# Attention on one Trainium2 core: the output projection as three fp32r passes over high and low parts, its tiles spread over two groups

## The chip, the cores and the metric

The kernel runs on one core of one Trainium2 chip. The metric is device time in microseconds for one execution, inputs and outputs in DRAM. TensorE (PE), VectorE (DVE), ScalarE (ACT), GpSimd (POOL) and SyncE (SP, which only issues DMAs here) run side by side, each through its own list of instructions in order, and wait for one another by semaphores.

## The reference

A macaron block on x of 2 x 2048 rows of 512 floats: half a mixture-of-experts layer, attention, half a mixture-of-experts layer, each behind a layer norm and added to x. Only the attention is touched:

```python
q = (x @ Wq + bq).reshape(b, s, 16, 32).transpose(0, 2, 1, 3)
k = x @ Wk + bk                      # one head of 32 for all 16 query heads
v = x @ Wv + bv
attn = softmax(einsum('bhsd,btd->bhst', q, k) / sqrt(32), axis=-1)
out = einsum('bhst,btd->bhsd', attn, v).transpose(0, 2, 1, 3).reshape(b, s, 512)
return out @ Wo + bo
```

## The kernel before

Attention is one unrolled program (`attention`). The 4096 rows are 8 chunks c of QT = 512 queries; the 16 heads are GPC = 4 groups g of HG = 4 heads. G = 4c + g counts the 32 groups. A group goes over its batch's 2048 keys in STEPS = 16 steps of 128, two steps to a pair (phase) p = 0 to 7.

In phase p TensorE makes eight score blocks (`scores`, L1776, fp32r, 128 keys x 512 queries of a head) and, in turn with them, eight blocks of the row maxima of the groups to come (`maxima`, L1797, fp32r). Then follow, where they are due, the transposed shifts (L1815, phase 6), an output tile (`output`, L1807), the denominators (L1836, phase 4), and at the end of the phase the values of the two steps before (`values`, L1825, fp32, into pO). Block maxima, shifts, output tiles and denominators take turns in pM, a ring of RING = 4 PSUM banks: each waits in `bank_free` until the bank's user four places earlier has been read. With eight maxima a phase, a shift, a tile or a denominator is a phase's ninth bank user and waits for the fifth maximum of its phase.

ACT takes the exponential of each score block (L1744). POOL adds the probabilities of two steps in two halves of 128x1024, both inputs in SBUF (`add_pair`, L1691), and between the halves of most pairs issues a DMA that accumulates the sum of an earlier pair (`bring`, L1707). In pair 1 it also normalises the output of the group before the last one (L1720). DVE reduces each block maximum out of PSUM (L1914), and at the end of its phase does, in this order of the code: copy_o (L1941, phase 0: pO of the group before to SBUF), make_shifts (phase 5: L1924 and L1925 reduce the maxima to one value a row, one in fp32 and one rounded to fp32r; L1928 subtracts the two, 128x16, all in SBUF), copy_shift (phase 6), the addition of an output tile to xo (L1919), the denominators' copy (phase 4) and their reciprocal (phase 6). The shifts go through the transposes of phase 6 into qT of the next group.

A chunk's output is four tiles of 128 rows, each the sum over the four groups of o_n[g] (fp32, 128x128 weights) times Wo[g] (128x512). They stand in the group g = 1 of the next chunk, in phases 4 to 7. The tiles of the last chunk (`last_output`, L1857) come at the end of the program. SP stores a finished chunk and loads the next rows (`store_x`, `load_x`) in the group g = 2, ahead of the DMAs that carry the denominators (`reciprocals`).

Numbers such as "(1,6)" below mean group g = 1, phase 6. The query projection ahead of attention (L1268 to L1270) already multiplies by three fp32r passes: high x high, low x high, high x low.

Of the kernel before, what the change touches and what calls it, by code (L numbers as in the profile page):

```python
# [38 lines left out]
def begin(eng, *sems):  # L39
    for s in sems:  # L40
        eng.sem_inc(s, A)  # L41
# [1391 lines left out]
def attention(nc, tag, k, prep, wo, q_d, d_d, sums, xb_d, x_out):  # L1433
# [8 lines left out]
    with ExitStack() as ctx:  # L1442
# [40 lines left out]
        FIRST_BLOCKS = (11, 11, 11, 11, 10, 10)  # L1483
        OUT_PAIRS = (4, 5, 6, 7)
        SUM_PAIR = 4
# [13 lines left out]
        pair = [m.sb(f"pair{b}", [P, HG * QT]) for b in range(MOVED)]  # L1499
        o_new = m.sb("o_new", [P, QT])  # L1500
        o_n = [m.sb(f"o_n{g}", [P, QT]) for g in range(GPC)]
        d_sb = m.sb("d", [P, QT])
# [9 lines left out]

        s_wo = m.sem("wo")
        s_xl = m.sem("xl")
        s_xs = m.sem("xs")
# [25 lines left out]

        def o_raw(g):
            return o_new if g == 0 else o_n[g]

        def blocks_in(G, k):
# [9 lines left out]
        def output_in(G, k):  # L1555

            return OUT_PAIRS.index(k) if G % GPC == 1 and G > GPC and k in OUT_PAIRS else None

# [29 lines left out]
        def last_out(t):  # L1588

            return pM[:, (END + t) % RING, :] if t < RING - 1 else pS[:, 0, :]  # L1590
# [4 lines left out]
        with nc.Block() as block:  # L1595
# [66 lines left out]
            def _(pool):  # L1662
# [47 lines left out]
                def normalise(c, g):  # L1710
                    G = GPC * c + g
                    pool.wait_ge(s_oc, A + G + 1)
                    pool.sem_inc(k["pool_on"], 1)
                    pool.wait_ge(s_ri, A + 64 * (G + 1))
                    pool.sem_inc(k["pool_on"], 1)
                    if g == 0 and not (isinstance(c, int) and c == 0):

                        pool.wait_ge(s_mr, A + outputs_done[c - 1])
                        pool.sem_inc(k["pool_on"], 1)
                    pool.tensor_tensor(o_n[g][:, :], o_raw(g)[:, :], d_rec[:, :], ALU.mult).then_inc(s_on, 1)  # L1720

# [11 lines left out]
            def _(act):  # L1733
                begin(act, s_ex, s_sha)

# [10 lines left out]
                def copy_shift(G, g, h):  # L1746
                    if h == 2:
                        act.wait_ge(s_x, A + G + 1)
                    act.activation(qT[g][3 * DH:4 * DH, h, :], pM[h * DH:(h + 1) * DH, shift_at[G] % RING, :], ACT.Copy
                                   ).then_inc(s_sha, 1)  # L1750

                for h in (2, 3):
                    copy_shift(0, 0, h)
                for G in range(GROUPS):
                    for t in range(STEPS):
                        for h in range(HG):
                            exponential(G, t, h)
                        if t == 2 * COPY_PAIR + 1 and G + 1 < GROUPS:
                            for h in (2, 3):
                                copy_shift(G + 1, (G + 1) % GPC, h)  # L1760

            @block.tensor
            def _(pe):
# [36 lines left out]
                def output(r, c, t):  # L1800

                    bank_free(r)
                    if t == 0:
                        pe.wait_ge(s_wo, A + 16)
                        pe.wait_ge(s_on, A + GPC * (c + 1))
                    for g in range(GPC):
                        ins = pe.matmul(pM[:, r % RING, :], o_n[g][:, t * P:(t + 1) * P], wo_sb[:, g, :],  # L1807
                                        start=g == 0, stop=g == GPC - 1)
                    ins.then_inc(s_mp, 1)
# [38 lines left out]
                def last_output(t, groups):  # L1848

                    if t == HG - 1 and 0 in groups:  # L1850
                        pe.wait_ge(s_ex, A + GROUPS * (STEPS * HG))
                    if t == 0 and 0 in groups:
                        pe.wait_ge(s_on, A + GROUPS - 1)
                    if GPC - 1 in groups:
                        pe.wait_ge(s_lon, A + t + 1)
                    for g in groups:
                        ins = pe.matmul(last_out(t), o_n[g][:, t * P:(t + 1) * P], wo_sb[:, g, :], start=g == 0,  # L1857
                                        stop=g == GPC - 1)
                    if GPC - 1 in groups:
                        ins.then_inc(s_mp, 1)  # L1860

# [46 lines left out]
            def _(dve):  # L1908
                begin(dve, s_mr, s_mx, s_shift, s_shd, s_dc, s_rec, s_oc, s_lrec, s_lon)

# [27 lines left out]
                def copy_o(c, g):  # L1938

                    dve.wait_ge(s_pv, A + (GPC * c + g + 1) * STEPS)  # L1940
                    dve.tensor_copy(o_raw(g)[:, :], pO[:, :]).then_inc(s_oc, 1)  # L1941

# [11 lines left out]
                def phase(G, p):  # L1954
# [5 lines left out]
                    if p == 0 and G > 0:  # L1960
                        copy_o(*divmod(G - 1, GPC))
                    if p == SHIFT_PAIR and G + 1 < GROUPS:
                        make_shifts(G + 1, count)
# [17 lines left out]
                for G in range(GROUPS):  # L1981
                    for p in range(PAIRS):
                        phase(G, p)
                dve.wait_ge(s_lsum, A + PAIRS)
                dve.wait_ge(s_ri, A + 64 * (GROUPS - 1))
# [3 lines left out]
                def last_quarter(t):  # L1989
# [3 lines left out]
                    if t == 0:  # L1993
                        dve.wait_ge(s_pv, A + GROUPS * STEPS)
                    dve.tensor_tensor(o_n[GPC - 1][:, part], pO[:, part], d_rec[:, part], ALU.mult).then_inc(s_lon, 1)

# [73 lines left out]
```

## Time and profile before

| | us |
|---|---|
| median of 3 runs | 3182.35 (3176.6 to 3187.31) |
| the profiled execution | 3182.29 |
| its span, first to last instruction | 3180.6 |
| attention in it | about 820 to 2509 |
| TensorE busy, of the span | 2770.0 (87%) |
| POOL | 2218.7 (70%) |
| DVE | 2046.3 (64%) |
| ACT | 1522.7 (48%) |

The shares of the whole span mix three stages. In attention TensorE is busy nearly throughout; the experts before and after it are bound otherwise and are not touched. A matmul record lasts from its start to the end of its way through the array, so records that follow each other overlap: the distance of their starts is what one costs.

### The profile page before, as it was taken

To read this page: it belongs to the slowest core of one execution; us is meant where nothing else is said; L and a number is where in the kernel's file an instruction comes from. 1 tells how busy PE (TensorE), PEld (TensorE's weight loads), DVE (VectorE), ACT (ScalarE), POOL (GpSimd) and SP (SyncE) were. 2 spreads that over 40 slices of the span, in tenths; PEclk is the share of its full clock that TensorE was granted. 3 is DMA by queue.
4 is the path that set the end of the run, shared out by engine and by line. 5 is a ranking of instruction groups with operands and counts; after the bars stand their busy time and mean duration, and the time that the engine had idled before them with its cause. 6 is when DMAs were issued, how large, how long until landed. Compare 5 with 4: busy or idle time off the path is not lost. (4 is left out here: it accounts for less than half of the span.)

```text
span 3180.6 us, 44938 instructions
## 1 busy us (share of the span) xinstructions
PE 2770.0 (87%) x15264; PEld 1651.1 (52%) x15264; DVE 2046.3 (64%) x3922; ACT 1522.7 (48%) x2871; POOL 2218.7 (70%) x1430
## 2 busy tenths in 40 slices
PE   7967777388899999999999999999999776888870
PEld 4644444166455555555555555555554464555540
DVE  7843222267788878788787887887874394333334
ACT  5522222153466656566566665665656351222220
POOL 2248888462489879799798897997978323777770
PEclk9978888689999999999999999999999877999995
DMA  5669999895377777678676776776766364999998
GB/s 211 220 198 244 237 241 242 184 272 189 83 157 161 144 159 147 137 170 160 143 162 134 167 144 139 164 150 155 148 135 140 121 219 135 212 236 240 236 184 322
DMA packets 216987, 575.78 MB, mean 181 GB/s; under 512 B 33980, under 2 KB 35004, under 8 KB 192824
## 3 DMA queue, kind: packets, MB, share of 16 engines
q0 software_dynamic: 87296, 343.98, 53.7%
q1 hardware_dynamic: 125240, 220.55, 21.4%
q10 hardware_dynamic: 4224, 8.39, 0.7%
q8 instruction: 123, 2.02, 0.3%
q14 instruction: 104, 0.85, 0.1%
HBM read 230.94 MB, written 155.24 MB: 121 GB/s over the span
## 5 line engine op out<-in xcount | busy, mean ns | idle before, releaser
L1914 DVE TENSOR_REDUCE attention_mx<-attention_pM 128x1 f32<-128x512 f32 x1984 | 1209.3, 682 | 197.0 <-PE attention_pM L1797 196.3
L1744 ACT ACTIVATE attention_prob<-attention_pS 128x512 f32<-128x512 f32 x2048 | 1032.7, 624 | 592.2 <-PE attention_pS L1776 591.8
L1691 POOL TENSOR_TENSOR attention_pair<-attention_prob 128x1024 f32<-128x1024 f32 x380 | 949.6, 2504 | 210.0 <-ACT attention_prob L1744 199.3
L1776 PE MATMUL attention_pS<-attention_qT,prep_kT 128*128 128x512 f32 x2048 | 840.6, 412 | 3.1 <-ACT attention_prob L1744 2.2
L1797 PE MATMUL attention_pM<-prep_kT,attention_qT 96*128 96x512 f32 x1984 | 788.2, 398 | 1.8 <-DVE attention_mx L1914 1.1
L1776 PEld LDWEIGHTS attention_pS<-attention_qT,prep_kT 128*128 128x128 f32 x2048 | 387.5, 190 | 308.9 <-issue 210.2
L1825 PE MATMUL attention_pO<-attention_prob,attention_v 128*32 128x512 f32 x4096 | 491.7, 598 | 0.0
L768 POOL DMA_INDIRECT sum<-experts_res,c_table x256 | 403.7, 1577 | 125.4 <-issue 79.4
L1797 PEld LDWEIGHTS attention_pM<-prep_kT,attention_qT 96*128 96x128 f32 x1984 | 377.9, 190 | 92.0 <-DVE attention_mx L1914 16.5
L752 POOL DMA_INDIRECT experts_rows<-xn_rows,c_table x256 | 250.7, 979 | 103.8 <-issue 70.1
L797 PE MATMUL experts_pT<-c_ident,experts_rows 128*128 128x128 f32 x1024 | 169.8, 307 | 120.8 <-issue 46.8
L943 DVE TENSOR_SCALAR experts_res<-experts_pD,experts_rows 128x512 f32<-128x512 f32 x128 | 93.5, 749 | 272.8 <-DMA sum<-experts_res,c_table 173.4
L1825 PEld LDWEIGHTS attention_pO<-attention_prob,attention_v 128*32 128x32 f32 x4096 | 110.1, 109 | 252.4 <-issue 155.6
L1691 POOL TENSOR_TENSOR prep_acc<-attention_prob 128x1024 f32<-128x1024 f32 x68 | 165.7, 2449 | 88.6 <-ACT attention_prob L1744 84.1
L797 PEld LDWEIGHTS experts_pT<-c_ident,experts_rows 128*128 128x128 f32 x1024 | 141.0, 209 | 155.8 <-issue 105.4
L922 DVE COPY experts_xT<-experts_pT 128x512 f32<-128x512 f32 x128 | 88.3, 690 | 198.7 <-PE experts_pT L797 133.5
L892 ACT ACTIVATE experts_res<-experts_pD,experts_rows 128x512 f32<-128x512 f32 x128 | 85.3, 686 | 257.6 <-DMA sum<-experts_res,c_table 191.2
L309 POOL TENSOR_TENSOR route_eqp<-route_eq,route_count 128x1536 f32<-128x1536 bf16 (+1 forms) x16 | 48.2, 3012 | 201.7 <-ACT route_count L429 201.7
L1691 POOL TENSOR_TENSOR attention_acc<-attention_prob 128x1024 f32<-128x1024 f32 x64 | 156.7, 2473 | 6.5 <-POOL attention_pair L1691 3.5
L884 ACT ACTIVATE experts_sg<-experts_pU 128x256 f32<-128x256 f32 x80 | 30.7, 384 | 267.8 <-PE experts_pU L814 119.8
L878 ACT ACTIVATE experts_xT<-experts_pT 128x512 f32<-128x512 f32 x128 | 76.5, 597 | 108.4 <-PE experts_pT L797 63.3
L814 PE MATMUL experts_pU<-experts_xT,experts_wup 128*64 128x256 f32 x1024 | 123.2, 395 | 1.0 <-issue 1.0
(181 smaller groups left out, 3135.1 us busy)
## 6 DMA issues: line engine op xcount, KB each, us to landing
prep_acc<-attention_pair POOLq DMA_DIRECT2D x96, 1024.0 KB, 7.6
attention_acc<-attention_pair POOLq DMA_DIRECT2D x90, 1024.0 KB, 7.3
attention_qT<-q_parts SPq DMA_DIRECT2D x96, 256.0 KB
xn_rows<-route_xn SPq DMA_DIRECT2D x16, 1152.0 KB, 6.6
experts_wup<-in_L_ffn_w_up_dram SPq DMA_DIRECT2D x64, 256.0 KB
q_parts<-prep_acc SPq DMA_DIRECT2D x64, 256.0 KB, 4.3
ahead_wup<-in_L_ffn_w_up_dram SPq DMA_DIRECT2D x64, 256.0 KB, 9.0
combine_got<-sum SPq DMA_DIRECT2D x16, 1024.0 KB
```

The costliest lines, as they stand in the source:

```text
L752: pool.indirect_dma_start(rows[e % RING][:, a * HALVES + h, :], None, xn_d, bass.IndirectOffsetOnAxis(ap=k["table"][:, 2 * e + a, h:h + 1] ...
L768: pool.indirect_dma_start(sums[a], bass.IndirectOffsetOnAxis(ap=k["table"][:, 2 * e + a, h:h + 1], axis=0), res[e % 2][:, a, h, :], None, ...
L797: t = pe.transpose(pT[:, half, o:o + P], rows[e % RING][:, a * HALVES + h, c:C:CK], k["ident"][:, :])
L814: t = pe.matmul(pU[n % 2][a * H:(a + 1) * H, v, :], wts[b][0][:, a, c, v * H:(v + 1) * H], xT[e % 2][:, c, a, :], start=c == 0, stop=c == ...
L922: dve.tensor_copy(xT[e % 2][:, 2:4, a, :], pT[:, 1, :].rearrange("p (c n) -> p c n", c=2)).then_inc(s_cd, 1)
L943: dve.tensor_scalar(res[e % 2][:, 1, h, :], pD[:, h, 1, :], rows[e % RING][:, HALVES + h, C + 2 * e + 1:C + 2 * e + 2], None, ALU.mult).th ...
L1691: pool.tensor_tensor(to[:, part], prob[2 * n % PROBS][:, part], prob[(2 * n + 1) % PROBS][:, part], ALU.add).then_inc(s_pair, 1)
L1744: act.activation(prob[t % PROBS][:, h * QT:(h + 1) * QT], pS[:, at, :], ACT.Exp).then_inc(s_ex, 1)
L1776: pe.matmul(pS[:, n % 3, :], kT[:, key:key + P], qT[g][:, h, :], start=True, stop=True).then_inc(s_sc, 1)
L1797: pe.matmul(pM[:, r % RING, :], qT[g][0:3 * DH, h, t * P:(t + 1) * P], kT[0:3 * DH, key:key + 512], start=True, stop=True).then_inc(s_mp, 1)
L1825: ins = pe.matmul(pO[h * DH:(h + 1) * DH, :], v_sb[:, batch * STEPS + t, :], prob[t % PROBS][:, h * QT:(h + 1) * QT], start=t == 0, stop=t ...
L1914: dve.tensor_reduce(mx[:, unit, part:part + 1], pM[:, r % RING, :], X, ALU.max).then_inc(s_mr, 1)
```

## The change

o and Wo are each split into a high part (rounded to fp32r by ACT) and a low part (the rest, subtracted by DVE and rounded to fp32r). An output tile becomes, for each of four groups, high x high + low x high + high x low, 12 fp32r matmuls in place of 4 fp32 ones. Wo is split once, in the groups G = 1 and 2. The normalised o of group G - 2 is split in group G, high after the exponentials of pair 4, low behind the maxima of phase 5 ahead of the shifts. The four tiles stand at (1,6), (1,7), (2,0), (2,1) instead of (1,4) to (1,7). copy_o writes into one of two buffers `raw` and waits for POOL's normalising of two groups before; POOL normalises in place and no longer waits for the outputs of the chunk before, which ACT now does. At the end the first three groups of a tile are split, the last one stays fp32.

```diff
@@ -1481,7 +1481,8 @@
         FIRST_BLOCKS = (11, 11, 11, 11, 10, 10)
-        OUT_PAIRS = (4, 5, 6, 7)
+        OUT_PAIRS = ((1, 6), (1, 7), (2, 0), (2, 1))
+        HIGH_PAIR, LOW_PAIR = 4, 5
         SUM_PAIR = 4
@@ -1497,8 +1498,12 @@
         pair = [m.sb(f"pair{b}", [P, HG * QT]) for b in range(MOVED)]
-        o_new = m.sb("o_new", [P, QT])
-        o_n = [m.sb(f"o_n{g}", [P, QT]) for g in range(GPC)]
+        raw = [m.sb(f"raw{b}", [P, QT]) for b in range(2)]
+        o_hi = [prep[n][:, :, :].rearrange("p c n -> p (c n)") for n in ("wkvh", "wkvl")]
+        o_hi += [m.sb(f"o_hi{b}", [P, QT], F32R)[:, :] for b in range(2)]
+        wo_hi, wo_lo = prep["wqh"], prep["wql"]
+        o_lo = [m.sb(f"o_lo{g}", [P, QT], F32R) for g in range(GPC)]
+        o_last = m.sb("o_last", [P, QT])
         d_sb = m.sb("d", [P, QT])
@@ -1554,7 +1560,8 @@
-            return OUT_PAIRS.index(k) if G % GPC == 1 and G > GPC and k in OUT_PAIRS else None
+            at = (G % GPC, k)
+            return OUT_PAIRS.index(at) if G > GPC + 1 - (at[0] == 1) and at in OUT_PAIRS else None
@@ -1713,11 +1720,7 @@
                     pool.sem_inc(k["pool_on"], 1)
-                    if g == 0 and not (isinstance(c, int) and c == 0):
-
-                        pool.wait_ge(s_mr, A + outputs_done[c - 1])
-                        pool.sem_inc(k["pool_on"], 1)
-                    pool.tensor_tensor(o_n[g][:, :], o_raw(g)[:, :], d_rec[:, :], ALU.mult).then_inc(s_on, 1)
+                    pool.tensor_tensor(raw[G % 2][:, :], raw[G % 2][:, :], d_rec[:, :], ALU.mult).then_inc(s_on, 1)
@@ -1748,6 +1751,18 @@
                                    ).then_inc(s_sha, 1)
+
+                def high_wo(g):
+                    if g == 0:
+                        act.wait_ge(s_wo, A + 16)
+                    act.activation(wo_hi[:, g, :], wo_sb[:, g, :], ACT.Copy).then_inc(s_woh, 1)
+
+                def high(G):
+                    c, g = divmod(G, GPC)
+                    act.wait_ge(s_on, A + G + 1)
+                    if c > 0:
+                        act.wait_ge(s_mr, A + outputs_done[c - 1])
+                    act.activation(o_hi[g], raw[G % 2][:, :], ACT.Copy).then_inc(s_oh, 1)
@@ -1755,9 +1770,14 @@
                             exponential(G, t, h)
+                        if G == 1 and t % 2 == 1 and t < 2 * GPC:
+                            high_wo(t // 2)
+                        if t == 2 * HIGH_PAIR + 1 and G > 1:
+                            high(G - 2)
                         if t == 2 * COPY_PAIR + 1 and G + 1 < GROUPS:
                                 copy_shift(G + 1, (G + 1) % GPC, h)
+                high(GROUPS - 2)
@@ -1801,11 +1821,14 @@
                     if t == 0:
-                        pe.wait_ge(s_wo, A + 16)
-                        pe.wait_ge(s_on, A + GPC * (c + 1))
+                        pe.wait_ge(s_wol, A + GPC)
+                        pe.wait_ge(s_ol, A + GPC * (c + 1))
+                    own = slice(t * P, (t + 1) * P)
                     for g in range(GPC):
-                        ins = pe.matmul(pM[:, r % RING, :], o_n[g][:, t * P:(t + 1) * P], wo_sb[:, g, :],
-                                        start=g == 0, stop=g == GPC - 1)
+                        pe.matmul(pM[:, r % RING, :], o_hi[g][:, own], wo_hi[:, g, :], start=g == 0, stop=False)
+                        pe.matmul(pM[:, r % RING, :], o_lo[g][:, own], wo_hi[:, g, :], start=False, stop=False)
+                        ins = pe.matmul(pM[:, r % RING, :], o_hi[g][:, own], wo_lo[:, g, :], start=False,
+                                        stop=g == GPC - 1)
                     ins.then_inc(s_mp, 1)
@@ -1849,15 +1872,18 @@
                         pe.wait_ge(s_ex, A + GROUPS * (STEPS * HG))
+                    own = slice(t * P, (t + 1) * P)
                     if t == 0 and 0 in groups:
-                        pe.wait_ge(s_on, A + GROUPS - 1)
-                    if GPC - 1 in groups:
-                        pe.wait_ge(s_lon, A + t + 1)
+                        pe.wait_ge(s_ol, A + GROUPS - 1)
                     for g in groups:
-                        ins = pe.matmul(last_out(t), o_n[g][:, t * P:(t + 1) * P], wo_sb[:, g, :], start=g == 0,
-                                        stop=g == GPC - 1)
-                    if GPC - 1 in groups:
-                        ins.then_inc(s_mp, 1)
+                        if g < GPC - 1:
+                            pe.matmul(last_out(t), o_hi[g][:, own], wo_hi[:, g, :], start=g == 0, stop=False)
+                            pe.matmul(last_out(t), o_lo[g][:, own], wo_hi[:, g, :], start=False, stop=False)
+                            pe.matmul(last_out(t), o_hi[g][:, own], wo_lo[:, g, :], start=False, stop=False)
+                        else:
+                            pe.wait_ge(s_lon, A + t + 1)
+                            pe.matmul(last_out(t), o_last[:, own], wo_sb[:, g, :], start=False, stop=True
+                                      ).then_inc(s_mp, 1)
@@ -1937,8 +1963,22 @@
-                    dve.wait_ge(s_pv, A + (GPC * c + g + 1) * STEPS)
-                    dve.tensor_copy(o_raw(g)[:, :], pO[:, :]).then_inc(s_oc, 1)
+                    G = GPC * c + g
+                    dve.wait_ge(s_pv, A + (G + 1) * STEPS)
+                    if G > 1:
+                        dve.wait_ge(s_on, A + G - 1)
+                        dve.sem_inc(k["dve_on"], 1)
+                    dve.tensor_copy(raw[G % 2][:, :], pO[:, :]).then_inc(s_oc, 1)
+
+                def low_wo(g):
+                    dve.wait_ge(s_woh, A + g + 1)
+                    dve.tensor_tensor(wo_lo[:, g, :], wo_sb[:, g, :], wo_hi[:, g, :].bitcast(F32), ALU.subtract
+                                      ).then_inc(s_wol, 1)
+
+                def low(G):
+                    dve.wait_ge(s_oh, A + G + 1)
+                    dve.tensor_tensor(o_lo[G % GPC][:, :], raw[G % 2][:, :],
+                                      o_hi[G % GPC].bitcast(F32), ALU.subtract).then_inc(s_ol, 1)
@@ -1959,6 +1999,10 @@
                         copy_o(*divmod(G - 1, GPC))
+                    if G == 2 and p < GPC:
+                        low_wo(p)
+                    if p == LOW_PAIR and G > 1:
+                        low(G - 2)
                     if p == SHIFT_PAIR and G + 1 < GROUPS:
@@ -1981,6 +2025,7 @@
                         phase(G, p)
+                low(GROUPS - 2)
                 dve.wait_ge(s_lsum, A + PAIRS)
@@ -1992,7 +2037,7 @@
                         dve.wait_ge(s_pv, A + GROUPS * STEPS)
-                    dve.tensor_tensor(o_n[GPC - 1][:, part], pO[:, part], d_rec[:, part], ALU.mult).then_inc(s_lon, 1)
+                    dve.tensor_tensor(o_last[:, part], pO[:, part], d_rec[:, part], ALU.mult).then_inc(s_lon, 1)
```

## Rows read from the trace of the kernel before

**Rows 1.** Windows view: busy us (count) by engine, granted clock, DMA share, GB/s
```profile
1200.00:1500.00 300.00, 300.00 (x1655) 169.37 (x1654) 252.19 (x427) 195.56 (x388) 259.30 (x137) 1.00 0.73 151
```

**Rows 2.** Source view of L1941, 1064 to 1284: count, ns, first to last start
```profile
L1941 DVE COPY attention_o_new<-attention_pO x1: 691/691/691, 1080.5 to 1080.5; 128x512 f32<-128x512 f32 x1
...
L1941 DVE COPY attention_o_n<-attention_pO x3: 691/692/692, 1143.6 to 1240.9; 128x512 f32<-128x512 f32 x3
```

**Rows 3.** Source view of L1807: weight loads of the output tiles
```profile
L1807 PEld LDWEIGHTS attention_pM<-attention_wo,attention_o_n x224: 186/190/190, 1101.7 to 2389.6; 128*128 128x128 f32 x112
```

**Rows 4.** Timeline (start us, us, what), TensorE: seven fp32r passes in a row
```profile
811.64 0.40 PE L1270 MATMUL attentionp_pQ<-attentionp_xh,prep_wql 128*128 128x512 f32 x1
...
813.04 0.40 PE L1270 MATMUL attentionp_pQ<-attentionp_xh,prep_wql 128*128 128x512 f32 x1
```

**Rows 5.** Timeline, TensorE: a tile of today, and an ordinary phase
```profile
1131.85 0.39 PE L1797 MATMUL attention_pM<-prep_kT,attention_qT 96*128 96x512 f32 x1
...
1132.15 3.70 PE L1807 MATMUL attention_pM<-attention_wo,attention_o_n 128*128 128x512 f32 x8
...
1143.77 0.40 PE L1797 MATMUL attention_pM<-prep_kT,attention_qT 96*128 96x512 f32 x1
...
1147.37 1.92 PE L1825 MATMUL attention_pO<-attention_prob,attention_v 128*32 128x512 f32 x16
```

**Rows 6.** Timeline, VectorE, at the end of phase 0 of a group 2
```profile
1143.57 0.69 DVE L1941 COPY attention_o_n<-attention_pO 128x512 f32<-128x512 f32 x1 [0.28 <-PE attention_pO L1825]
...
1144.21 4.88 DVE L1914 TENSOR_REDUCE attention_mx<-attention_pM 128x1 f32<-128x512 f32 x8
```

**Rows 7.** Groups by line and form: the last tiles, busy us, mean ns
```profile
L1857 PE MATMUL attention_pM<-attention_wo,attention_o_n 128*128 128x512 f32 x24 | 11.0, 601 | 0.0
```

**Rows 8.** Timeline, ScalarE, behind pair 4, with the idle time before
```profile
1168.86 4.03 ACT L1744 ACTIVATE attention_prob<-attention_pS 128x512 f32<-128x512 f32 x8 [3.48 <-PE attention_pS L1776]
```

**Rows 9.** Timeline of SyncE's DMA queue in a group 2
```profile
1144.88 0.43 SPq L1610 DMA_DIRECT2D sum<-attention_xo  x1
...
1156.29 0.38 SPq L1604 DMA_DIRECT2D attention_xo<-x_rows  x1
...
1167.46 1.26 SPq L1618 DMA_DIRECT2D d_parts<-attention_d  x4
```

**Rows 10.** Source view of L1366, a VectorE addition with two SBUF inputs
```profile
L1366 DVE TENSOR_TENSOR attentionp_got<-attentionp_got,attentionp_other x8: 681/688/1153, 625.7 to 647.6; 128x512 f32<-128x512 f32 x8
```

**Rows 11.** Timelines, VectorE then GpSimd, end of phase 5, usual group
```profile
1174.01 0.22 DVE L1924 TENSOR_REDUCE attention_whole<-attention_mx 128x16 f32<-128x64 f32 x1
...
1174.39 0.21 DVE L1928 TENSOR_TENSOR attention_shift<-attention_whole,attention_shift 128x16 f32<-128x16 f32 x1
...
1174.89 4.88 DVE L1914 TENSOR_REDUCE attention_mx<-attention_pM 128x1 f32<-128x512 f32 x8 [0.29 <-PE attention_pM L1797]
...
1172.18 2.38 POOL L1691 TENSOR_TENSOR attention_pair<-attention_prob 128x1024 f32<-128x1024 f32 x1 [1.91 <-ACT attention_prob L1744]
...
1175.09 2.70 POOL L1691 TENSOR_TENSOR attention_pair<-attention_prob 128x1024 f32<-128x1024 f32 x1
```

**Rows 12.** Timelines, VectorE, GpSimd, TensorE: phase 6 of G = 0; usual phase
```profile
866.14 2.38 DVE L1928 TENSOR_TENSOR attention_shift<-attention_whole,attention_shift 128x16 f32<-128x16 f32 x1
...
868.45 4.86 DVE L1914 TENSOR_REDUCE attention_mx<-attention_pM 128x1 f32<-128x512 f32 x8
...
865.80 2.67 POOL L1691 TENSOR_TENSOR attention_pair<-attention_prob 128x1024 f32<-128x1024 f32 x1
...
863.82 1.92 PE L1825 MATMUL attention_pO<-attention_prob,attention_v 128*32 128x512 f32 x16
...
872.16 1.92 PE L1825 MATMUL attention_pO<-attention_prob,attention_v 128*32 128x512 f32 x16
...
1172.26 1.92 PE L1825 MATMUL attention_pO<-attention_prob,attention_v 128*32 128x512 f32 x16
...
1178.61 1.92 PE L1825 MATMUL attention_pO<-attention_prob,attention_v 128*32 128x512 f32 x16
```

More of the change, by code:

```diff
@@ L1513, in attention @@
         s_wo = m.sem("wo")
+        s_woh = m.sem("woh")
+        s_wol = m.sem("wol")
+        s_oh = m.sem("oh")
+        s_ol = m.sem("ol")
         s_xl = m.sem("xl")
@@ L1540, in attention @@
         s_shd = m.sem("shd")
-        def o_raw(g):
-            return o_new if g == 0 else o_n[g]
         def blocks_in(G, k):
@@ L1733, in _ @@
             def _(act):
-                begin(act, s_ex, s_sha)
+                begin(act, s_ex, s_sha, s_woh, s_oh)
                 def exponential(G, t, h):
@@ L1908, in _ @@
             def _(dve):
-                begin(dve, s_mr, s_mx, s_shift, s_shd, s_dc, s_rec, s_oc, s_lrec, s_lon)
+                begin(dve, s_mr, s_mx, s_shift, s_shd, s_dc, s_rec, s_oc, s_lrec, s_lon, s_wol, s_ol)
                 def maxima(r, count, n):
```

## The prediction

> **What bounds the kernel now.** I read the stages first, then the groups inside attention, then one phase instruction by instruction. In a 300 us stretch of attention TensorE is busy for all 300 us at a granted clock of 1.00 (its 2.4 GHz level), POOL for 259, DVE for 252, ACT for 196 [rows 1]. So the matmul stream sets the time, and a microsecond taken from it counts only as long as nothing makes it wait. The copies of pO out of PSUM (L1941) mark the groups: 1080.5 to 1143.6 is the group that carries the four output tiles, 63.1 us; the next two take 97.3/2 = 48.65 us each [rows 2]. A tile therefore costs (63.1 - 48.65)/4 = 3.61 us of the bound today, and there are 224/8 = 28 such tiles in the groups (224 weight loads, one a record) [rows 3], besides four at the end.
>
> **The passes.** A tile is 8 matmul records now (an fp32 matmul runs as two) and 12 fp32r passes afterwards. fp32r passes stand back to back in the query projection: six starts in 813.04 - 811.64 = 1.40 us, 0.233 us each, though each record lists 0.40 [rows 4]. So 12 x 0.233 = 2.80 us. The tile also waits for its bank: the present one starts 0.30 us after the last block maximum instead of 0.233 [rows 5], 0.07 us; the weight load behind such a wait is in the open, somewhere between nothing and its 0.19 us [rows 3]. I take 0.08, near the low end, since a load normally runs ahead of its matmul. A tile then costs 2.95 us (2.80 to 3.06) and saves 0.66 us (0.55 to 0.81).
>
> **Moving tiles to group 2.** In (1,6), (1,7) and (2,0) nothing else is late, 0.66 each. At (2,0) DVE adds the tile only after copy_o, which waits for the phase's values, where copy_o is now followed at once by the next phase's maxima, 0.64 us later [rows 6]. With an addition in between (0.6 us, the distance of such instructions) and the new semaphore increment (0.06, my estimate, between 0 and 0.1) the maxima of phase 1 start 0.66 us late. TensorE makes a maximum every 0.467 us and DVE takes 4.88/8, about 0.6; four banks cover this within a phase, but the ninth bank user of the phase, the tile (2,1), waits for the fifth maximum: today 1144.21 + 4 x 0.6 + 0.69 = 1147.30 against 1147.37, when TensorE goes on [rows 5, 6]. There is no slack: what DVE loses there, TensorE loses. So (2,1) saves nothing. Per chunk 3 x 0.66 = 2.0, in seven chunks 13.9 us (0 lost there and 0.81 saved: 22.7; 0.55 and a loss of 0.2: 10). The last tiles run 24 of their 32 records as 36 passes: 24 records take 11.0 us today [rows 7], 36 x 0.233 are 8.4, at most 2.6 saved, less the changes between the two kinds; I take 1.3 (0 to 2.6).
>
> **The high parts on ACT.** One 128x512 copy at the end of pair 4 of each group from G = 2, about 0.6 us as ACT's eight exponentials take 4.03: ACT has 3.48 us idle right there [rows 8]. Cost nothing; without that cover 30 x 0.6 = 18 us. Its new wait for the chunk's earlier outputs, formerly POOL's, is met by pair 1 of group 2, three pairs before. Behind it only exponentials queue. The four of Wo, once, lie in idle time as well: ACT is busy for only 196 of 300 us [rows 1].
>
> **The queues.** SP's store of a chunk now waits for tile (2,1) rather than being ready when SP gets there. Today it is issued at 1144.88 and over by 1156.29, 11.4 us; SP is next needed for the denominators at 1167.46 [rows 9]. The tile's addition would come at about 1149.2 + 2 x 2.95 + 0.7 + 0.9 = 1156.7, the store end at 1168.1, while the denominators move by 6.6 to 1174.1. Six microseconds are left, cost nothing. POOL's normalising keeps its place and loses a wait that never came last.
>
> **The low parts on DVE: here the time goes.** low() is put behind the maxima of phase 5, ahead of make_shifts, in G = 2 to 30 (29 groups with a phase 6 that makes shifts). It is a subtraction of 128x512 with both inputs in SBUF; a like one takes 0.68 us unhindered [rows 10]. What matters is what POOL does then. In phase 5 the maxima end at about 1173.97, just ahead of L1924 at 1174.01; L1924, with one input, runs its 0.22 us in the middle of POOL's addition of 1172.18 to 1174.56; L1928, the only instruction there with two SBUF inputs, ends at 1174.60, 0.04 us after that addition [rows 11]. That might be chance, but in G = 0, whose phases bring more maxima, DVE comes later: L1928 comes at 866.14, POOL's addition has been running since 865.80 and ends at 868.47, and an instruction of 0.2 us takes 2.38 and ends at 868.52. The maxima behind it begin at 868.45, TensorE waits for a bank, and that phase lasts 872.16 - 863.82 = 8.34 us against 1178.61 - 1172.26 = 6.35 in a usual group [rows 12]: 1.99 us lost. Undisturbed, the maxima start 1174.89 - 1172.26 = 2.63 us after the values, here at 866.45: 2.00 late on DVE is 1.99 on TensorE. Phase 6 too has a ninth bank user, the transposes.
>
> Now the new order. low() is ready at about 1173.9, inside the addition that ends at 1174.56, and is held to about 1174.5; with 0.6 us to go it ends near 1175.1. L1924 and L1925 follow at about 1175.05 and 1175.2, L1928 is ready at 1175.4. POOL's second half addition starts at 1175.09 and lasts 2.70 [rows 11], perhaps 0.1 later because of low(). L1928 misses the gap of half a microsecond between POOL's two additions in which it gets through today, and ends at about 1177.85. The next maxima start near 1177.8 instead of 1174.89: 2.9 us late, all of it TensorE's. 29 x 2.9 = 84 us. Bounds: 2.0, the one case measured (58 us), and 3.1 if POOL itself is pushed back by 0.2 (90 us). I take 2.9, since it is read from the place itself.
>
> The Trainium skill, page "SBUF — State Buffer", section "Who interferes with whom", says of this that a VectorE instruction with two SBUF inputs contends with a GpSimd instruction that reads SBUF, and that whichever starts second is blocked to the end of the first. The rows above agree; read alone, the rule would let each of the two instructions wait up to a whole POOL addition, 29 x (2.4 + 2.7) = 148 us; the places of the rows make it 84.
>
> low_wo(), four times in G = 2, has two SBUF inputs too. By the same gaps I put 0.5 us on each, 2 us (0 to 8).
>
> **The sum**, against the profiled execution of 3182.3 us (its span is 3180.6; the median of the runs is 3182.35, so nothing is to be converted): 3182.3 - 13.9 - 1.3 + 84 + 2 = 3253 us. With the bounds: 3182.3 - 25.4 + 58 = 3215 and 3182.3 - 10 + 90 + 8 = 3270.
>
> **The rivals.**
> - B, L1928 still slips in ahead of POOL's second addition. It would have to be ready by 1175.1 instead of 1175.4. Then the shifts end near 1175.6 and the maxima come 0.66 us late: 29 x 0.66 = 19; 3182.3 - 15.2 + 19 + 2 = 3188 us. Against it: at 866.14 it was 0.34 us behind and was held [rows 12].
> - C, the other side: low() is not held at all, because two inputs are not what holds L1928. Then low() adds about 0.5 us, L1928 is ready at 1174.9, in the gap ahead of 1175.09, and the maxima start 0.22 late, after the 0.29 us that DVE idles there now [rows 11]: 6.4 us. 3182.3 - 15.2 + 6.4 + 1 = 3174 us. It decides at 1175.09. The end of L1928 with POOL's, at both places, speaks against it.
> - D, low() and the shifts cost nothing and the cheap end of the tiles holds: 3182.3 - 25 = 3157 us. The 0.29 us of idle time against a subtraction of 0.6 speaks against it.
> - E, low() is passed over at the first addition's end and both wait for the second: it ends at 1178.4, L1928 at 1178.95, 4.0 us late, 116 us; 3285 us. The gap of half a microsecond with low() already waiting speaks against it.
> - The passes could fail to be cheaper, at the 0.40 us that a record lists: 12 x 0.40 = 4.8 us, 28 x 1.2 = 34 us more. The starts in the query projection exclude that [rows 4].
>
> **How the numbers follow.** Forecast 0.76, B 0.08, C 0.07, D 0.04, E 0.05. The range takes in the forecast with its bounds and E: 3215 to 3286, 0.81 together. About 0.3% (9.5 us) is what a measurement can tell from no change. Slower by more is the forecast and E, 0.81. B and most of C lie within it, 0.13. D and the rest of C are faster, 0.06.
>
> **What would show it.** In the changed kernel the tile is 12 passes in about 2.8 us, the groups with tiles about 5 to 6 us longer than the others, all groups from G = 2 about 2.9 us longer in phase 6; L1928's successor takes over 2 us in nearly every group instead of 0.21 and ends with a POOL addition; TensorE, never idle before, waits about 1 us or more for a maximum in each phase 6. If L1928 stays at 0.2 us, the main term is wrong and B, C or D holds. If the subtraction itself shows over 2 us, it is E.

## The result

The changed kernel takes 3262.1 us (median, 3254.7 to 3267.6) against 3183.4 for the kernel before: ratio 1.0248, 95% interval 1.0221 to 1.0276. The forecast was 3253 us, in a range of 3215 to 3286, and slower with a chance of 0.81. The profiled execution's span is 3262.0 us against 3180.6.

The profile's page and the views that group waits and lines already name the place. These are the page's line of busy times; the group of the block maxima on TensorE, busy us and mean ns, then the idle time before and its releaser; the group of the shifts' subtraction on DVE; and the wait as a total with its count and longest case:

```profile
PE 2802.7 (86%) x15388; PEld 1688.7 (52%) x15388; DVE 2147.4 (66%) x3957; ACT 1551.6 (48%) x2906; POOL 2218.6 (68%) x1430
...
L1817 PE MATMUL attention_pM<-prep_kT,attention_qT 96*128 96x512 f32 x1984 | 808.1, 408 | 59.4 <-DVE attention_mx L1940 58.7
...
L1954 DVE TENSOR_TENSOR attention_shift<-attention_whole,attention_shift 128x16 f32<-128x16 f32 x32 | 72.7, 2271 | 1.1
...
PE attention_pM L1817 <- DVE attention_mx L1940: 58.7, 30, 2.5
```

L1817 is the old L1797, L1940 the old L1914, L1954 the old L1928. TensorE, busy for all of a 300 us stretch before [rows 1], now waits 30 times for a block maximum: 1.15 us in G = 0, 2.47 in G = 2 behind the low part of Wo, and 1.96 to 1.97 in phase 6 of each of G = 2 to 29; and the subtraction of 128x16, 0.21 us in a usual group before [rows 11], takes 2.27 us on average. One such place, the end of phase 5 in G = 7, as timelines (start us, us, what) of DVE, POOL and TensorE:

```profile
1241.35 1.22 DVE L1980 TENSOR_TENSOR attention_o_lo<-attention_raw,prep_wkvl 128x512 fp32r<-128x512 f32 x1
1242.49 0.20 DVE L1950 TENSOR_REDUCE attention_whole<-attention_mx 128x16 f32<-128x64 f32 x1
1242.61 0.21 DVE L1951 TENSOR_REDUCE attention_shift<-attention_mx 128x16 fp32r<-128x64 f32 x1
1242.86 2.40 DVE L1954 TENSOR_TENSOR attention_shift<-attention_whole,attention_shift 128x16 f32<-128x16 f32 x1
1245.18 4.86 DVE L1940 TENSOR_REDUCE attention_mx<-attention_pM 128x1 f32<-128x512 f32 x8
...
1239.64 2.37 POOL L1698 TENSOR_TENSOR attention_pair<-attention_prob 128x1024 f32<-128x1024 f32 x1 [1.91 <-ACT attention_prob L1747]
1241.96 0.85 POOL L1714 DMA_DIRECT2D attention_acc<-attention_pair  x1
1242.55 2.65 POOL L1698 TENSOR_TENSOR attention_pair<-attention_prob 128x1024 f32<-128x1024 f32 x1
...
1239.72 1.92 PE L1848 MATMUL attention_pO<-attention_prob,attention_v 128*32 128x512 f32 x16
...
1245.91 0.50 PE L1817 MATMUL attention_pM<-prep_kT,attention_qT 96*128 96x512 f32 x1 [1.96 <-DVE attention_mx L1940]
...
1248.89 1.92 PE L1848 MATMUL attention_pO<-attention_prob,attention_v 128*32 128x512 f32 x16
```

Set beside rows 11 and 12: the low part (L1980) is ready while POOL's first addition runs and takes 1.22 us instead of about 0.68. The shifts' subtraction then comes after the first addition's end (1242.01) and ends at 1245.26, 0.06 us after the second one's. The maxima start at 1245.18; 2.63 us after the values, as in a usual group before, would have been 1242.35. Phase 6 lasts 1248.89 - 1239.72 = 9.17 us against 6.35 before [rows 12]: 2.82 us lost. L1951, which writes as small a tile but has one input, runs its 0.21 us while the second addition runs; only the subtraction with two inputs is held.

The distance of the copies of pO measures a group, as in rows 2. In the changed kernel (L1971) a usual group and then one with tiles, by first and last start:

```profile
L1971 DVE COPY attention_raw<-attention_pO x2: 692/692/692, 1043.4 to 1094.9; 128x512 f32<-128x512 f32 x2
...
L1971 DVE COPY attention_raw<-attention_pO x2: 692/692/692, 1094.9 to 1155.3; 128x512 f32<-128x512 f32 x2
```

Values in us, read from the starts of the copies in DVE's timeline (groups in which the granted clock stayed at 1.00, but for G = 2 and e4's g = 2):

| kernel | usual group | with tiles, g = 1 | g = 2 | G = 2 |
|---|---|---|---|---|
| before | 48.7 | 63.07 | 48.7 | 48.68 |
| changed | 51.5 | 60.34 | 55.15 | 58.29 |
| e2_shifts_first | 48.90 | 57.78 | 52.55 | 53.37 |
| e4_subtraction_alone | 51.5 | 63.07 | 52.40 | 52.40 |
| f0_split_one_phase_earlier | 48.69 | 57.54 | 52.34 | 53.81 |
| f1_tiles_apart | 48.69 | 57.51 | 51.74 | 53.83 |
| f3_wo_on_pool | 48.69 | 57.51 | 51.73 | 48.84 |

In e4 the granted clock fell to half behind the wait of phase 6 in each of the groups G = 2, 6, 10, 14, 18, 22 and 26 and in no other; with this go the 0.9 us by which its g = 2 lies above its usual group. In the changed kernel the groups G = 1 to 30 together are 85.3 us longer than before, what lies ahead of them is 1.7 us shorter, and the end of attention, from the last copy of pO to the last addition to xo, is 2.1 shorter: 81.5 of the span's 81.4.

### The profile page after: what moved, and what is told of

It is laid out like the page before. It is cut to its first block and busy times, and to the rows that moved or that the text cites. A ratio compares the mean times of both kernels' runs of the same rounds, so it can differ in the third digit from the quotient of the medians.

```text
span 3262.0 us, 45309 instructions
## 1 busy us (share of the span) xinstructions
PE 2802.7 (86%) x15388; PEld 1688.7 (52%) x15388; DVE 2147.4 (66%) x3957; ACT 1551.6 (48%) x2906; POOL 2218.6 (68%) x1430
## 5 line engine op out<-in xcount | busy, mean ns | idle before, releaser
L1747 ACT ACTIVATE attention_prob<-attention_pS 128x512 f32<-128x512 f32 x2048 | 1043.5, 623 | 632.8 <-PE attention_pS L1796 632.0
L1940 DVE TENSOR_REDUCE attention_mx<-attention_pM 128x1 f32<-128x512 f32 x1984 | 1208.7, 683 | 191.1 <-PE attention_pM L1817 190.6
L1817 PE MATMUL attention_pM<-prep_kT,attention_qT 96*128 96x512 f32 x1984 | 808.1, 408 | 59.4 <-DVE attention_mx L1940 58.7
L1817 PEld LDWEIGHTS attention_pM<-prep_kT,attention_qT 96*128 96x128 f32 x1984 | 381.0, 192 | 184.9 <-DVE attention_mx L1940 112.9
```

Of the source, the lines that this page charges most:

```text
L1747: act.activation(prob[t % PROBS][:, h * QT:(h + 1) * QT], pS[:, at, :], ACT.Exp).then_inc(s_ex, 1)
L1817: pe.matmul(pM[:, r % RING, :], qT[g][0:3 * DH, h, t * P:(t + 1) * P], kT[0:3 * DH, key:key + 512], start=True, stop=True).then_inc(s_mp, 1)
L1940: dve.tensor_reduce(mx[:, unit, part:part + 1], pM[:, r % RING, :], X, ALU.max).then_inc(s_mr, 1)
```

## The experiments

The theory: while an addition of POOL with both inputs in SBUF runs, a DVE instruction with two SBUF inputs is held. The low part is held to the end of the first addition, which makes the shifts' subtraction miss its way past POOL, and it is held to the end of the second. The rivals: the 0.6 us of DVE work as such; the place of the split; the passes and their tiles. The diffs show the lines that matter; the allocation of spare tiles and code that only moves along are left out.

**e4: the subtraction alone.** The kernel before, with nothing of the change but a subtraction of the same size into a spare tile:

```diff
+                    if p == SHIFT_PAIR and G > 1:
+                        dve.wait_ge(s_wo, A + 16)
+                        dve.tensor_tensor(spare[:, :], wo_sb[:, 0, :], wo_sb[:, 1, :], ALU.subtract)
                     if p == SHIFT_PAIR and G + 1 < GROUPS:
                         make_shifts(G + 1, count)
```

> The kernel before with one thing added: in phase 5 of G = 2 to 31, ahead of the shifts, a DVE subtraction of 128x512 with two inputs in SBUF into a spare tile. Nothing else of the change. Theory: in the 22 groups without tiles the shifts' subtraction takes 2.3 us and TensorE loses 2.9 us: 64 us; in the 7 groups with tiles phase 5 carries a tile, whose time covers the wait; 3182 + 64 = 3246 us, some more if the clock falls behind the waits. Rival (passes, split on ACT, moved tiles are the cause): 3182 us.

3245.3 us against 3177.1 for the kernel before in the same series: ratio 1.0217 (1.0200 to 1.0234). The groups of DVE's lines, count, busy us and mean ns:

```profile
L1929 DVE TENSOR_TENSOR attention_shift<-attention_whole,attention_shift 128x16 f32<-128x16 f32 x32 | 72.8, 2274 | 1.1
...
L1965 DVE TENSOR_TENSOR attention_spare<-attention_wo 128x512 f32<-128x512 f32 x30 | 38.1, 1268 | 0.1
```

The two instructions last as in the changed kernel. Usual groups grow by 2.82 us, the groups with tiles by nothing: there the subtractions are held just as long (1.19 and 2.42 us at 1121.30 and 1122.79), but the tile at (1,5) gives DVE the time. With nothing else of the change the kernel loses 68 us, most of the change's 79.

**e2: the same work, behind the shifts.**

```diff
-                    if p == LOW_PAIR and G > 1:
-                        low(G - 2)
                     if p == SHIFT_PAIR and G + 1 < GROUPS:
                         make_shifts(G + 1, count)
+                    if p == LOW_PAIR and G > 1:
+                        low(G - 2)
```

> The changed kernel with the low part still in phase 5, but behind the shifts instead of ahead of them; the same DVE work ahead of the maxima of phase 6. Theory: the shifts' subtraction gets through at the end of POOL's first addition as before (0.2 us), the low part follows in the gap ahead of the second addition and ends about 0.35 us after TensorE's next maximum is ready; 29 x 0.35 = 10 us, 3182 - 15 + 7 + 10 = 3184 us. Rival (DVE's 0.6 us more of work in front of phase 6 is the cause, not POOL): no better than the change, 3250 to 3265 us.

3174.6 us, ratio to before 0.9992 (0.9983 to 1.0002). The same place, DVE then POOL:

```profile
1273.04 0.22 DVE L1954 TENSOR_TENSOR attention_shift<-attention_whole,attention_shift 128x16 f32<-128x16 f32 x1
1273.17 0.68 DVE L1980 TENSOR_TENSOR attention_o_lo<-attention_raw,attention_o_hi 128x512 fp32r<-128x512 f32 x1
1273.78 4.86 DVE L1940 TENSOR_REDUCE attention_mx<-attention_pM 128x1 f32<-128x512 f32 x8
...
1270.84 2.37 POOL L1698 TENSOR_TENSOR attention_pair<-attention_prob 128x1024 f32<-128x1024 f32 x1 [1.91 <-ACT attention_prob L1747]
1273.15 0.86 POOL L1714 DMA_DIRECT2D prep_acc<-attention_pair  x1
1273.74 2.70 POOL L1698 TENSOR_TENSOR attention_pair<-attention_prob 128x1024 f32<-128x1024 f32 x1
```

The shifts' subtraction waits at the first addition's end and gets through (0.22 us), and the low part straight behind it goes too, unheld at 0.68 us. A usual group is 48.90 us, 0.20 longer than before, not the 0.35 that I had expected. By the medians 87 us of the changed kernel's time come from the order of two instructions (81 by the two ratios, since the time of the kernel before differs between the series; 88 by the lengths of the groups G = 1 to 30 in the traces). The rival of the DVE work as such falls.

**e3: one SBUF input in the low part's place.**

```diff
-                    dve.tensor_tensor(o_lo[G % GPC][:, :], raw[G % 2][:, :],
-                                      o_hi[G % GPC].bitcast(F32), ALU.subtract).then_inc(s_ol, 1)
+                    dve.bn_stats(one[:, :], raw[G % 2][:, :]).then_inc(s_ol, 1)
```

> The changed kernel with the subtraction of the low part of o replaced by an instruction of the same length with one input in SBUF (row statistics of the same tile), at the same place; the low part of o is left out of the result (its tiles are filled once). Theory: it isn't held, takes 0.68 us, the shifts' subtraction is ready at about 0.15 us ahead of POOL's second addition and takes 0.2 us; maxima 0.2 us late, 29 x 0.2 = 6; 3182 - 15 + 7 + 6 = 3180 us. Rival (DVE's time alone): as the change, 3250 to 3265 us. If the shifts' subtraction just misses the gap, its rows show 2.3 us and the time is near 3255 us.

3261.4 us, ratio 1.0265 (1.0248 to 1.0282): no better. DVE, then POOL, in G = 8; then the same around a low part of Wo in G = 2:

```profile
1295.21 0.68 DVE L1981 BATCH_NORM_STATS2 attention_one<-attention_raw 128x6 f32<-128x512 f32 x1
...
1296.17 2.96 DVE L1955 TENSOR_TENSOR attention_shift<-attention_whole,attention_shift 128x16 f32<-128x16 f32 x1
...
1293.50 2.37 POOL L1699 TENSOR_TENSOR attention_pair<-attention_prob 128x1024 f32<-128x1024 f32 x1 [1.91 <-ACT attention_prob L1748]
1295.82 0.86 POOL L1715 DMA_DIRECT2D prep_acc<-attention_pair  x1
1296.41 2.67 POOL L1699 TENSOR_TENSOR attention_pair<-attention_prob 128x1024 f32<-128x1024 f32 x1
...
955.36 0.68 DVE L1976 TENSOR_TENSOR prep_wql<-attention_wo,prep_wqh 128x512 fp32r<-128x512 f32 x1
...
952.95 2.38 POOL L1699 TENSOR_TENSOR attention_pair<-attention_prob 128x1024 f32<-128x1024 f32 x1 [2.85 <-ACT attention_prob L1748]
955.27 0.85 POOL L1715 DMA_DIRECT2D prep_acc<-attention_pair  x1
```

One half of the theory holds: with one input the instruction runs its 0.68 us in the middle of an addition. The other half is wrong as I had it. The shifts' subtraction is ready 0.30 us after the first addition's end (1295.87) and 0.24 us before the second one's start, and is held all the same. So the gap between the additions, in which POOL issues a DMA, is not open to an instruction that arrives so late in it. It is at its very start: the rows at 955 are of the same run, and there a low part of Wo comes 0.03 us after an addition's end, in a gap with an issue, and is not held (0.68 us). Delay alone is then enough to lose at this place, whatever it consists of, if it takes the subtraction 0.3 us past the end of the first addition.

**e1: the split one phase earlier, behind the denominators' copy.**

```diff
-        HIGH_PAIR, LOW_PAIR = 4, 5
+        HIGH_PAIR = 3
-                    if p == LOW_PAIR and G > 1:
-                        low(G - 2)
                     if p == SUM_PAIR and G > 0:
                         copy_d(r, count, G - 1)
+                    if p == SUM_PAIR and G > 1:
+                        low(G - 2)
```

> The changed kernel with the splitting of o one phase earlier: the high part behind pair 3, the low part on DVE at the end of phase 4 behind the denominators' copy, where POOL is between two additions and DVE then idles 1.7 us. Theory (POOL's running addition holds a DVE instruction with two SBUF inputs): the subtraction takes about 0.7 us, the subtraction of the shifts is back at 0.2 us, groups without tiles at 48.7 us as before the change; 3182 - 15 for the tiles + 7 for Wo = 3174 us. Rival (the 12 passes and their bank waits cost the time, wherever the split stands): stays at 3255 to 3265 us.

3291.7 us, ratio 1.0361 (1.0343 to 1.0378): my expectation was off by over 100 us, and for the same reason as in e3. DVE, then POOL:

```profile
1288.99 3.25 DVE L1980 TENSOR_TENSOR attention_o_lo<-attention_raw,attention_o_hi 128x512 fp32r<-128x512 f32 x1
1292.17 4.86 DVE L1940 TENSOR_REDUCE attention_mx<-attention_pM 128x1 f32<-128x512 f32 x8
...
1297.45 2.75 DVE L1954 TENSOR_TENSOR attention_shift<-attention_whole,attention_shift 128x16 f32<-128x16 f32 x1
...
1288.40 0.87 POOL L1714 DMA_DIRECT2D prep_acc<-attention_pair  x1
1289.00 2.69 POOL L1698 TENSOR_TENSOR attention_pair<-attention_prob 128x1024 f32<-128x1024 f32 x1
```

The low part arrives in the gap, while the DMA issue still runs and 0.01 us ahead of the second addition's start, and waits for the whole of that addition, 3.25 us. The maxima of phase 5 start late, the shifts come late in turn and are held as well: two waits a group.

**e5 and e6: is it the DMA issue that closes the gap?** As e3, with pair 5's DMA issue moved behind the second addition and a gap made of semaphore counts only, of three widths:

```diff
+                        if n == SHIFT_PAIR and not last:
+                            if f == 0:
+                                pool.wait_ge(s_pair, A + G * STEPS + (2 * n + 1))
+                                for _ in range(12):   # 5 in e6_gap_short, 3 in e6_gap_shorter
+                                    pool.sem_inc(k["pool_on"], 1)
+                            else:
+                                bring(c, g, n - 1)
```

> As e3_one_input (low part of o left out), but in pair 5 POOL's DMA issue stands behind the second addition, and between the two additions POOL only counts a semaphore up twelve times. Theory A (the DMA issue between the additions closes the way): the shifts' subtraction, ready about 0.3 us after the first addition's end, now gets through, 0.2 us instead of 2.96, and the time falls from 3261 to about 3175 us. Theory B (the second addition claims it well ahead of its recorded start): it stays held if the gap is not much over 0.3 us, about 3260 us; the rows tell how long the gap was.

> As e5_gap_without_dma (low part of o left out), with five counts between the two additions in place of twelve: a gap of about 0.5 to 0.6 us without a DMA issue, as wide as the one with the DMA issue in e3_one_input, where the shifts' subtraction came 0.24 us ahead of the second addition's recorded start and was held. Theory A (the DMA issue closes the way): it gets through, 0.2 us, about 3167 us. Theory B (the second addition claims its port at least 0.24 us ahead of its recorded start): held, 2.7 us and more, about 3250 us.

> As e6_gap_short, with three counts: a gap of about 0.4 us, the shifts' subtraction ready some 0.1 us ahead of the second addition's recorded start. Theory A: it gets through as long as it is ready before that start, 0.2 us, 3167 us. Theory B: held, about 3250 us.

One run of each gave 3166.5, 3172.7 and 3169.7 us; e3 had 3261.4. The shortest gap, DVE then POOL; then, from the same run, a low part of Wo in a gap with a DMA issue; last, all shifts' subtractions of this run and of e3, with their shortest, median and longest time in ns:

```profile
1275.30 0.20 DVE L1962 TENSOR_TENSOR attention_shift<-attention_whole,attention_shift 128x16 f32<-128x16 f32 x1
...
1272.63 2.38 POOL L1699 TENSOR_TENSOR attention_pair<-attention_prob 128x1024 f32<-128x1024 f32 x1 [1.90 <-ACT attention_prob L1755]
1275.44 2.40 POOL L1699 TENSOR_TENSOR attention_pair<-attention_prob 128x1024 f32<-128x1024 f32 x1 [0.43 <-POOL attention_pair L1699]
...
934.72 3.44 DVE L1983 TENSOR_TENSOR prep_wql<-attention_wo,prep_wqh 128x512 fp32r<-128x512 f32 x1
...
934.35 0.86 POOL L1722 DMA_DIRECT2D attention_acc<-attention_pair  x1
...
L1962 DVE TENSOR_TENSOR attention_shift<-attention_whole,attention_shift x32: 186/193/1979, 819.6 to 2422.6; 128x16 f32<-128x16 f32 x32
...
L1955 DVE TENSOR_TENSOR attention_shift<-attention_whole,attention_shift x32: 190/2954/2972, 816.6 to 2512.1; 128x16 f32<-128x16 f32 x32
```

Ready 0.14 us ahead of the second addition, nearer than in e3, it gets through in 0.20 us, as in every group from G = 1 on; the one long case, 1.98 us in G = 0, came 0.46 us after the second addition's start. A second addition that always claims its way well ahead of its start would have held it. The low part of Wo, 0.31 us behind an addition (of 932.03 to 934.41) whose gap still has its issue, is held in the same run. So the DMA issue in the gap makes the difference: with it, an instruction with two SBUF inputs that comes 0.24 us (e6_gap_short, 3.54 us at 934.20) or more after the first addition's end waits to the end of the addition behind; one that already waited when the first addition ended is let through, and so is one right behind it (e2; 0.03 us after the end in e3). What holds it stays open: the issue itself, the transfer that it starts and that moved along in e5 and e6, or the second addition already lined up behind the issue. That it isn't the issue alone is suggested by e2, where the low part runs its 0.68 us beside an issue of the usual 0.86.

**f0, f1, f3: what the change is worth without the wait.** f0 changes one line, so that the low part already waits when the addition of phase 4 ends:

```diff
-        HIGH_PAIR, LOW_PAIR = 4, 5
+        HIGH_PAIR, LOW_PAIR = 3, 4
```

> The changed kernel with one line other: the high part behind pair 3, the low part at the end of phase 4, ahead of the denominators' copy rather than behind it. POOL's first addition of the pair is then running and ends about 0.5 us later. Theory (an instruction that already waits when POOL's addition ends gets through, one that comes after it waits for the next addition): the low part takes about 1.2 us, the copy of the denominators comes 0.8 us later into 1.7 us of idle time, the shifts' subtraction is back at 0.2 us, groups without tiles at 48.7; 3177 - 14 + 7 = 3170 us. Rival (any place in phase 4 loses, as behind the copy): 3250 to 3292 us.

3167.1 us against 3176.0 before, ratio 0.9973 (0.9963 to 0.9982). DVE, then POOL, at the end of phase 4 and of phase 5:

```profile
1263.74 1.22 DVE L1980 TENSOR_TENSOR attention_o_lo<-attention_raw,attention_o_hi 128x512 fp32r<-128x512 f32 x1
1264.88 0.68 DVE L1986 COPY attention_d<-attention_pM 128x512 f32<-128x512 f32 x1
1266.46 4.88 DVE L1940 TENSOR_REDUCE attention_mx<-attention_pM 128x1 f32<-128x512 f32 x8 [0.90 <-PE attention_pM L1817]
...
1271.75 0.21 DVE L1954 TENSOR_TENSOR attention_shift<-attention_whole,attention_shift 128x16 f32<-128x16 f32 x1
...
1262.03 2.38 POOL L1698 TENSOR_TENSOR attention_pair<-attention_prob 128x1024 f32<-128x1024 f32 x1 [0.18 <-POOL attention_pair L1698]
```

The low part is held as long as in the changed kernel, 1.22 us, but 0.9 us of idle time remain behind it and the shifts' subtraction is where it was. So here the wait of the held instruction costs nothing.

f1 also moves the tiles apart:

```diff
-        OUT_PAIRS = ((1, 6), (1, 7), (2, 0), (2, 1))
+        OUT_PAIRS = ((1, 5), (1, 6), (1, 7), (2, 1))
```

> As f0_split_one_phase_earlier, and the four tiles at (1,5), (1,6), (1,7), (2,1) instead of (1,6), (1,7), (2,0), (2,1), so that no tile's addition on DVE stands between copy_o and the maxima of a phase with a tile. Theory: 0.7 us less in each of 7 chunks, 5 us less than f0, 3165 us. Rival (the second tile of group 2 is dear for another reason): as f0.

3162.6 us, ratio 0.9956 (0.9942 to 0.9970), 4.6 us below f0 by the medians: group 2 falls from 52.34 to 51.74 us, 0.6 in each of seven chunks.

f3 puts the low part of Wo on POOL:

```diff
-                    if G == 2 and p < GPC:
-                        low_wo(p)
+                        if G == 1 and n in (1, 4, 5, 7):   # POOL, behind add_pair(c, g, n)
+                            low_wo((1, 4, 5, 7).index(n))
```

> As f1_tiles_apart, and the low part of Wo, four subtractions, on POOL in G = 1 instead of DVE in G = 2. Theory: group 2 falls from 53 to 48.7 us, 4 to 5 us less than f1, 3160 us. Rival (POOL's extra 1.3 us a piece holds up the exponentials in G = 1): as f1.

3157.0 us, ratio 0.9940 (0.9923 to 0.9957): 0.6% below the kernel before. G = 2 falls from 53.83 to 48.84 us, and G = 1 stays at 48.68.

## Why the prediction was right

The forecast's one large term was right in place, size and sign: the measured time lies 9 us above the point. What it had wrong is small, and said with each term.

- **Passes and tiles.** A tile was put at 2.95 us and a chunk's saving at 2.0. In e2 the three tiles at (1,6), (1,7), (2,0) take (57.78 - 48.90)/3 = 2.96 us each, and a chunk saves (14.37 - 8.88 - 3.65) = 1.84, 13 us in seven chunks against 13.9. In the trace of the change the second tile of its group takes 2.98 us, start to start:

```profile
1362.70 0.50 PE L1828 MATMUL attention_pM<-prep_wqh,prep_wkvh 128*128 128x512 f32 x1
...
1365.68 1.92 PE L1848 MATMUL attention_pO<-attention_prob,attention_v 128*32 128x512 f32 x16
```

  That the tile (2,1) saves nothing, since DVE comes late out of phase 0, held: 3.65 us in e2, and 0.6 us less in f1, where no tile stands in phase 0.
- **The low part.** Forecast 2.9 us in each of 29 groups, 84 us; measured 2.82 in those with the clock at 1.00, and in 28 groups, 79 us. G = 30 should not have been counted: its phase 6 has no block maxima that could come late, and in e4 it grew by 0.4 us only (47.80 against 47.40). The order of the steps (held low part, missed gap, late maxima, late TensorE) is that of the rows above. One reason in it was wrong: I had the shifts' subtraction miss the gap by coming after the start of POOL's second addition. It would have been held 0.24 us ahead of that start too (e3). The result was the same, since it came 0.31 us behind it; but the border at 1175.09 that rivals B and C go by was wrong, and C, in which the subtraction lands in the gap and costs 6 us, was mis-priced: with the low part unheld e3 still lost as much as the change. C's own mechanism, that two inputs are not what holds, is excluded by e3's 0.68 us beside e4's 1.27.
- **What the Trainium skill says of it.** The Trainium skill, page "SBUF — State Buffer", section "Who interferes with whom", was right here on which instructions contend (two inputs held, one input not). The same section infers that descriptor generation and a tensor_tensor don't meet, as they use different interfaces of the shared pair. The rows of e2 agree: the low part takes its unheld 0.68 us while the issue takes its usual 0.86. That one which comes later into a gap with an issue is held (e3 against e6) doesn't by itself speak against it, since the second addition may already hold the place there; no run here tells.
- **Wo.** Put at 2 us (0 to 8); f3 against f1 gives 5.6 by the medians and 5.0 by the length of G = 2. In the changed kernel itself G = 2 is 58.29 - 51.5 = 6.8 us longer than a usual group, two falls of the clock in it included. Mis-sized, inside its bounds: three of the four low parts took 1.10, 1.21 and 3.44 us on DVE instead of the 0.68 of one that is not held.
- **The end.** Put at -1.3, it was -2.1.
- **What was missing: the clock.** In 12 of the 27 groups G = 3 to 29 the granted clock fell to half its level behind the wait in phase 6, and these groups are 0.7 to 1.35 us longer still, 12 us together. In the trace before TensorE waited once for over a microsecond behind the start of attention, 1.1 us in phase 6 of G = 0 (so "never idle before" was not quite right), and the clock stayed at 1.00; I didn't ask what a wait of two microseconds in every group would do to it.

With 2 us less ahead of the groups, which has nothing to do with the change, the terms are 3182 - 13 + 79 + 7 + 12 - 2 - 2 = 3263 for the profiled execution, against 3264 (3182.3 + 81.4). That the point lies only 9 us off is in part luck: the term for the low part was 5 us too large, while the clock and Wo brought 17 us that the sum did not have.

ACT's copies, the moved store and POOL's changed waits cost nothing, as put: f3, with all of them, has its usual groups at the 48.69 us of before.

## What to carry to other kernels

Before a two-input instruction on VectorE is added beside a busy GpSimd, read what GpSimd does at that moment, and above all which later two-input instruction loses its place: here the added one could cost nothing and the next one an entire GpSimd instruction. Such an instruction went through cheaply where it already waited when a GpSimd addition ended, and dearly where it came 0.24 us or more into a gap in which GpSimd issued a DMA. When a change disappoints, put the suspected instruction alone into the old kernel, and move it by one place in the new one: these two runs named the cause here.

## What the runs showed of the hardware that was not expected

With a DMA issue of GpSimd in it, the gap of some 0.54 us between two of its additions was closed to a VectorE instruction with two SBUF inputs that came 0.3 us or more after the first one's end (2.96 us in e3, 3.25 in e1), and open to one that came 0.03 us after it (0.68 us in e3), while a gap of 0.43 us without an issue was open up to 0.14 us ahead of the next addition (0.20 us in e6_gap_shorter).

TensorE's granted clock fell to half, 1.2 GHz, behind a wait of about 2 us in some groups and not in others. Windows of 2 us (busy us and count by engine, then granted clock, DMA share, GB/s), first behind the wait in G = 8, then behind the same wait in G = 7:

```profile
1297.00:1299.00 2.00, 1.60 (x6) 0.90 (x6) 2.00 (x4) 0.82 (x2) 0.00 (x0) 1.00 0.96 197
1299.00:1301.00 2.00, 2.00 (x11) 1.06 (x13) 2.00 (x5) 1.03 (x3) 1.96 (x1) 0.61 0.33 66
1301.00:1303.00 2.00, 2.00 (x12) 0.43 (x12) 1.91 (x4) 1.12 (x2) 2.00 (x3) 0.53 0.35 74
1303.00:1305.00 2.00, 2.00 (x14) 1.12 (x7) 0.81 (x2) 0.80 (x2) 1.60 (x1) 1.00 0.98 197
...
1247.00:1249.00 2.00, 1.90 (x13) 1.02 (x15) 2.00 (x5) 1.47 (x4) 1.45 (x1) 1.00 0.65 131
1249.00:1251.00 2.00, 2.00 (x17) 0.56 (x17) 1.94 (x4) 1.18 (x2) 2.00 (x3) 1.00 0.00 0
```

In G = 8 TensorE had been waiting until 1297.40 and ran on at 1.00, its 2.4 GHz level, for some 2 us before the clock fell; it was back at 1.00 some 3.4 us later. The values behind it took 2.90 us instead of 1.92. The wait in G = 7 was as long, to 0.01 us. In e1, where no wait of TensorE from G = 3 on is longer than 1.52 us, the clock fell in 13 of the groups G = 3 to 29. Why the one was followed by a fall and the other not stays open.
